# Which of two waits rides on the score scatter: a graph-and-feed-forward kernel on one Trainium2 core

## What is computed

```python
hr_src = h_r[:, src]
hr_dst = h_r[:, dst]
diff = hr_dst - hr_src
score = s_src + s_dst + jnp.einsum('hed,hd->he', diff, a_dif) + jnp.einsum('hed,hd->he', jnp.abs(diff), a_abs) + jnp.einsum('hed,hd->he', hr_src * hr_dst, a_prd)
alpha = jax.nn.leaky_relu(score, negative_slope=ALPHA)
m = jax.ops.segment_max(alpha_t, src, num_segments=N)
ex = jnp.exp(alpha_t - m[src])
denom = jax.ops.segment_sum(ex, src, num_segments=N)[src]
out = jax.ops.segment_sum(msg, src, num_segments=N)
```

## Time and profile before

| | us |
|---|---|
| median of 3 runs | 2567.65 |
| lowest and highest | 2567.59, 2571.53 |
| the profiled execution | 2566.56 |
| its span in the trace | 2564.8 |

### The profile page before, as it was taken

How to read it: one execution, slowest core, us unless ns; L and a number is a source line. 1 busy time by engine, 2 the same in 40 slices (tenths; PEclk the granted TensorE clock), 3 DMA queues, 4 the chain that set the end, 5 groups by cost and what they waited for, 6 DMA issues and landing times.

```text
span 2564.8 us, 22909 instructions
## 1 busy us (share of the span) xinstructions
PE 2226.7 (87%) x7917; PEld 1258.5 (49%) x7917; DVE 1095.5 (43%) x2478; ACT 728.3 (28%) x1206; POOL 539.8 (21%) x474
## 2 busy tenths in 40 slices
PE   6798864888999798879798898899798889999998
PEld 3476543676445453334454454455345454444443
DVE  8786662896323323344453354335325430000002
ACT  1475542775321110002151142124115011111111
POOL 4676642443210100010101101100110120012201
PEclk9899886897999789988899899899899989999999
DMA  9432234221021100022102101200301057777742
GB/s 376 109 59 43 42 80 99 63 56 50 1 86 66 50 0 19 1 85 90 49 1 61 59 0 47 72 0 0 115 10 43 15 211 298 300 288 299 296 189 64
DMA packets 61468, 243.14 MB, mean 95 GB/s; under 512 B 23183, under 2 KB 25699, under 8 KB 39244
## 3 DMA queue, kind: packets, MB, share of 16 engines
q1 hardware_dynamic: 31866, 174.12, 19.2%
q0 software_dynamic: 26336, 62.19, 8.0%
q10 hardware_dynamic: 3168, 5.63, 0.6%
HBM read 209.96 MB, written 31.92 MB: 94 GB/s over the span
## 4 chain that ended last, share of the span: by engine, by line
PE 55%; DVE 16%; issue 13%; DMA 7%; ACT 4%; POOL 3%; PEldq 0%; PEld 0%; SPq 0%; DVEq 0%; POOLq 0%; ACTq 0%
PE PS L724 18%; PE PS L731 10%; PE PS L1221 6%; PE PS L1230 6%; PE PS L1259 6%; DMA pair_scores<-TS,SIDX 5%; DVE ST L1893 1%; PE PS L1020 1%; POOL pair_scores L1754 1%; DVE Y L1901 1%; DVE AR L2184 1%; PE PS L1239 1%; PE PS L769 1%; DVE Y L2454 1%; DVE Y L2455 1%
## 5 line engine op out<-in xcount | busy, mean ns | idle before, releaser
L724 PE MATMUL PS<-XT,WR 128*128 128x113 f32 (+2 forms) x1264 | 363.6, 448 | 9.6 <-ACT XT L1327 7.6
L1725 POOL TENSOR_TENSOR RSTD<-VE,HALF 125x1 f32<-125x1 f32 x105 | 73.6, 701 | 1144.0 <-DVE VE L1896 1144.0
L724 PEld LDWEIGHTS PS<-XT,WR 128*128 128x128 f32 (+1 forms) x1264 | 199.7, 196 | 182.2 <-issue 180.1
L870 PE MATMUL PS<-HR,HOT 125*125 125x512 f32 x800 | 219.0, 423 | 47.5 <-DVE HOT L2041 47.5
L731 PE MATMUL PS<-WR,XT 128*125 128x512 f32 (+1 forms) x480 | 214.6, 601 | 6.6 <-ACT XT L1653 4.3
L2628 DVE TENSOR_TENSOR AR<-AR,PS 128x512 f32<-128x512 f32 (+1 forms) x44 | 30.3, 688 | 404.0 <-PE PS L1230 404.0
L724 PE MATMUL PS<-AR 125*128 125x512 f32 (+3 forms) x680 | 193.5, 439 | 9.3 <-ACT AR L1625 3.9
L870 PEld LDWEIGHTS PS<-HR,HOT 125*125 125x125 f32 x800 | 152.1, 198 | 91.3 <-DVE HOT L2041 40.6
L1918 DVE TENSOR_TENSOR AR<-PS,AR 125x512 f32<-125x512 f32 x55 | 38.1, 692 | 311.5 <-PE PS L731 311.0
L731 PE MATMUL PS<-WR,AR 128*125 128x512 f32 (+1 forms) x370 | 157.2, 576 | 10.3 <-ACT AR L1658 4.6
L724 PEld LDWEIGHTS PS<-AR 125*128 125x128 f32 (+1 forms) x680 | 106.1, 189 | 98.0 <-issue 89.1
(11 more groups left out here) (392 smaller groups left out, 3669.5 us busy)
## 6 DMA issues: line engine op xcount, KB each, us to landing
WR<-in_qkv SPq DMA_DIRECT2D x12, 1024.0 KB
WR<-in_omm SPq DMA_DIRECT2D x12, 1024.0 KB
pair_scores<-CNT SPq DMA_DIRECT2D x1, 12212.0 KB, 56.0
AR<-pair_scores SPq DMA_DIRECT2D x5, 2187.5 KB
AR<-in_x_a SPq DMA_DIRECT2D x10, 1024.0 KB, 9.7
AR<-in_x_b SPq DMA_DIRECT2D x10, 1024.0 KB, 4.8
AR<-in_x_c SPq DMA_DIRECT2D x10, 1024.0 KB, 7.0
WR<-in_x_a SPq DMA_DIRECT2D x8, 1024.0 KB, 8.9
```

What stands on the lines that cost most here:

```text
L724: last = mm(s.ap[0:parts, c0:c1], lhs(k), rhs(k)[:, c0:c1], start=(k == 0), stop=(k == terms - 1))
L870: last = mm(DIFF[m % 4], HOT[g % 2][0:P, k, tile(j)], HR[0:P, k, :, b, :], start=(k == 0 and b == 0), stop=(k == NT - 1 and b == 1))
L1725: g.tensor_tensor(RSTD[:, t:t + 1], VE[:, t:t + 1], HALF[:, :], ALU.pow)\
```

## The change

In put_scores the wait for the scores now stands behind the wait for the landing. The landing's wait, now written first, rides on the scatter, and the wait for the scores is the separate instruction. For m = 0 the same goes for the wait for the clearing of the table (scores_cleared). Nothing else is changed: the same instructions, buffers, semaphores and values, and PE, DVE, ACT and SP have the same instructions in the same order.

```diff
             def put_scores(m):
 
-                pool.wait_ge(score_ready, m + 1)
                 if m:
                     pool.wait_ge(scattered, 16 * m)
                 else:
                     pool.wait_ge(scores_cleared, 16)
+                pool.wait_ge(score_ready, m + 1)
                 g.indirect_dma_start(
```

## The result

| | before | after |
|---|---|---|
| median, us | 2570.81 (8 runs, 2561.18 to 2574.45) | 2552.26 (8 runs, 2541.00 to 2558.69) |
| the profiled execution, us | 2566.56 | 2558.69 |
| its span in the trace, us | 2564.8 | 2556.9 |

The ratio after to before is 0.9938 (95% interval 0.9925 to 0.9952). On 2570.81 us that is 15.9 us less, with 12.3 and 19.3 as the ends; the two medians lie 18.6 us apart. Forecast were 17 us less.

The account below looks back on a forecast made before the run. Landings of the pair_scores scatters bound the graph stage's tail. Savings 10.8 + 6.2 - 0.5 = 16.5 us, 17.4 with two unexplained starts, taken as 17: median 2567.65 to 2550.6 us, range 2543 to 2560.

Parts of the forecast that it names:

- The gap: Score scatters on POOL: landing to next start falls from 0.75 to 0.28 us, saving 0.47 us per landing-bound start.
- Rival (c): Score scatters: the riding wait holds POOL just as the separate one does, so no change, 2568 us; chance 0.05.
- The tail: Scatters m = 56 to 79, without pair_sums between them: 23 starts x 0.47 us = 10.8 us saved.
- The alternating part: Scatters m = 1 to 55, alternating with pair_sums: 6.2 us saved, less 0.5 us lost at m = 0.
- Rival (a): Alternating scatters: bulk loads eat the saving there, leaving 10.3 us in all, 2557.3 us; chance 0.12.
- The score wait: Made separate, it costs nothing for m = 1 to 79, hidden under a flight, and 0.48 us once at m = 0.
- The savings go through to the end: After the last scatter: DVE stays some 19 us ahead of the score load, so the scatters' saving reaches the end.
- everything behind 441 us should be as long as before: Stages from DVE's line 2165 on, after the score load: length unchanged; growth there would count against the prediction.
- The last reduction moves: DVE's last score reduction follows the landing 8 scatters before the end; idle before line 2165 shrinks by some 4 us.
- Rival (b): Behind the score load: shorter PE idle keeps its clock from staying low, 7 us more gained, 2543.6 us; chance 0.05.
- Scatter durations unchanged: Score scatters on POOL: their own times stay the same; a rise of half a microsecond would make the prediction wrong.
- rival (d): Earlier scatters fall onto other DVE instructions and lengthen: + 20 us, 2588 us, decided from a mean 0.47 us; chance 0.03.

Follow-up runs that it names:

- e3: The kernel before with the two waits swapped only for m = 0 to 55, old order in the tail: 2558.91 us (12 runs), ratio 0.9966.
- e8: The kernel before, unchanged, profiled a second time: 2565.89 us.
- e1: The changed kernel, unaltered, measured again beside before: 2548.71 us (6 runs), ratio 0.9923.
- e9: The changed kernel, unaltered, profiled a third time: 2549.36 us.
- e2: The kernel before with the two waits swapped only in the last 24 scatters (m = 56 to 79): 2558.63 us (7 runs), ratio 0.9967.
- e4: The changed kernel with the score wait, from m = 8, only before every fourth scatter, for four tiles at once: 2551.08 us (5 runs), ratio 0.9935.
- e6: The changed kernel plus a second separate, long-met wait (scores_cleared) written last, from m = 8: 2550.74 us (4 runs), ratio 0.9933.

## Why the prediction was right, step by step

The time (2552.26 against 2550.6), the range and the sign came out, and so did the mechanism. How closely is partly luck: the last scatter moved by 16.6 us in the profiled pair, but by 14.4 in the mean of the traces of before (2) and of the swap (3), and the two parts, timed one by one, gained 8.5 and 8.7 us where 10.8 and 5.7 were forecast. Their sum was better than what is known of each.

- **The gap, 0.75 to 0.28 us.** Right: 0.27 us measured. The pair_sums scatters and the first scatter of the kernel before were a good price list for the wait that rides. Rival (c), that the riding wait holds POOL just as long, falls with every trace of the swap. "Anatomy of one DMA" in "DMA: Bandwidth & Descriptors" of the Trainium skill has the wait end on the sequencer ahead of a dispatch of some 50 ns; the traces have 0.27 and 0.74 us from the landing to the start, both longer, and the difference between the two is not in it.
- **The tail, 10.8 us.** Right: from scatter 55 to the last it took 90.2 us in the mean of three traces with the old order there (before, e3, e8: 90.8, 91.0, 88.6) and 79.4 in six with the new one (after, e1, e9, e2, e4, e6: 79.0 to 79.8), 10.8 less. By time, e2 has 8.5 us for it (5.1 to 11.8).
- **The alternating part, 6.2 - 0.5 = 5.7 us.** About right: scatter 55 starts at 332.2 us in the mean with the old order there (before, e8, e2) and at 327.3 with the new (after, e1, e9, e3), 4.9 less, or 5.6 with e4 and e6 counted. It swings by several us between traces of one kernel (334.8 and 330.2 in the two of before); that this is the bulk loads falling on other scatters was not tested. Rival (a), that the loads eat this part, is ruled out by e3, which gains 8.7 us (5.4 to 12.3) with the swap in this part alone.
- **The score wait, nothing but 0.48 us at m = 0.** Right: 0.49 at m = 0, and nothing elsewhere, shown by the gap of 0.27 us in e4 (fewer of them) and e6 (more). One detail was off: between two scatters of the tail "no sequencer piece" was to be seen, and the chain of after has one, but it is the wait of the next scatter.
- **The savings go through to the end.** Right in the medians. The line that read "everything behind 441 us should be as long as before" failed in the profiled pair (2131.9 against 2123.5 us), and with it one of the signs by which the prediction was to be wrong (the stages behind 441 us grow). It isn't shown to be an effect of the change (e8, e9). It was too sharp a sentence for one trace of each: the rest varies by up to 8 us.
- **The last reduction moves, DVE's idle time down by some 4 us.** Off in size: 23.07 to 20.90, so 2.2 us, and it differs by more than that between traces of one kernel (19.7 to 23.3 in the three of the swap). Rival (b) built on it, that PE's clock comes back sooner, is not seen: the first 26 us had 0.56 in after and 0.69 in e9, two values that before has too (0.69 and 0.57).
- **POOL's idle time on landings about 75 us.** 77.8, near enough.
- **Scatter durations unchanged.** Nearly. The median is 987 ns in both, but the means rose. These are the page's groups after (busy us, mean ns, idle before):

```profile
L1743 POOL DMA_INDIRECT pair_sums<-CW,SIDX x80 | 134.8, 1686 | 56.8 <-DMA pair_sums<-CW,SIDX 25.1
...
L1754 POOL DMA_INDIRECT pair_scores<-TS,SIDX x80 | 88.8, 1110 | 94.7 <-DMA pair_scores<-TS,SIDX 77.8
```

In before they are 132.1 us (1651 ns) and 87.0 us (1088 ns): 2.7 + 1.8 = 4.5 us more in all, at most 35 ns a scatter. That is the direction of rival (d), far below the 0.47 us from which it would have decided. In the tail it can be seen at work, once for certain. POOL and DVE of after, then of before, in order of time:

```profile
392.10 2.47 DVE L2132 TENSOR_TENSOR WR<-CS,PRODUCT 64x1024 f32<-64x1024 f32 x2
393.48 1.93 POOL L1754 DMA_INDIRECT pair_scores<-TS,SIDX  x1 [1.40 <-DMA pair_scores<-TS,SIDX]
...
404.51 0.96 POOL L1754 DMA_INDIRECT pair_scores<-TS,SIDX  x1 [1.87 <-DMA pair_scores<-TS,SIDX]
404.82 2.47 DVE L2132 TENSOR_TENSOR WR<-CS,PRODUCT 64x1024 f32<-64x1024 f32 x2
```

In after a scatter starts just behind the start of the second of these two DVE instructions (393.35) and takes 1.93 instead of 0.96 us, and the next one starts 3.32 us after it instead of 2.35. With steps of 2.83 us, as in before, the pair fits between the start of one scatter and the next, and the scatter beside it takes 0.96 us. All seven traces with the new order in the tail have a step of 3.32 us at this pair, and the four with the old one have their usual 2.82 to 2.85. So the denser scatters pay some 0.97 us there, a term that the sum has at nothing. That the DVE instructions are the cause was not tested.

Not tried was what would go further, two score scatters in flight at a time: all of them write into one table, and edges with the same pair of nodes rely on the order.

## What to carry to other kernels

Where a scatter on POOL needs several waits, let the one that ends last ride on the scatter, and put those long met into the separate instructions: it was worth 0.47 us for each scatter that a landing releases, and the number of separate waits under a flight didn't matter. Which wait ends last is asked place by place (it was the other one at m = 0), and the chain shows it: 0.70 us of "issue" behind a sequencer piece is a late wait that stands separate. Judge what lies far behind an edit by the medians or by several traces, since after was 8 us longer there than before in one pair of traces and 4 us shorter in the next.

## What was not expected of the hardware

The 0.70 us behind a separate wait belong to POOL's scatter and not to separate waits as such. DVE's reduction also has a separate wait that ends with the same landings; this is the chain of before there:

```profile
366.14 0.03 issue
366.17 0.02 DVEq L2052
366.19 0.04 issue
366.23 0.70 DVE TS L2053
```

DVE starts 0.09 us after the landing (366.14 to 366.23), POOL's scatter 0.74 us after one. The waits of the swapped kernels further show that a separate wait, though met long before, isn't passed until the scatter ahead of it in POOL's queue is released: 406.35 in the chain of after, 0.03 us behind the landing that lets that scatter go, while the last reduction had ended at 391.6; and 396.94 in e4's, where the wait for m = 76 passes with the release of m = 75. What POOL does in the 0.70 us these runs don't show.
